# Layer-0 attention and feed-forward part joined in one block, normalisation per batch, and the opening of layer-1 attention reordered

## The chip, the core and the metric

One core of a Trainium2 chip runs the whole program. The metric is the device time of one execution in microseconds (us), the median of the runs shown. TensorE (PE in the rows) multiplies and transposes, VectorE (DVE) and ScalarE (ACT) do elementwise work, GpSimd (POOL) too, and SyncE (SP) issues the transfers from memory. Each has its own queue of instructions, worked through in order; semaphores tie the queues together.

## The reference

`x` is 8 batches of 128 tokens with 512 features. Four layers follow, each an attention part and a feed-forward part, each with a layer norm ahead of it and an addition behind:

```python
x = x + _L0_xattn_ref(_layernorm(x), ctx_4096, mask, position_bias, ...)   # 32 heads of 128
x = x + _L0_ffn_ref(_layernorm(x), W_org, lora_down, lora_up, lora_keys, Wq)
x = x + _L1_xattn_ref(_layernorm(x), ctx_4096, ctx_4096, Wq, Wk, Wv, Wo)   # 32 heads of 16, 8 for keys
x = x + _L1_ffn_ref(...)      # and two more layers
```

The feed-forward part of layer 0 projects the normalised x with `Wq`, takes the mean over the tokens of a batch, scores it against 8 keys, and uses the softmax of the scores as coefficients of 8 low-rank products (`lora_down`, `lora_up`), which are added to the dense product with `W_org`.

## The kernel before

Every operand of a large product is held as a high and a low part (`..._hi`, `..._lo`), and a product is three matmuls (`product`, lines 36 to 38). The high part is a rounding copy, mostly on ACT, the low part a subtraction on DVE or POOL.

`l0_attention` is one block with eight turns of four heads. In its last turn DVE also runs the last rounds of a ranking of the context (`rank_round`, `rank_end`) that only layer 2 needs. After the last turn PE makes the output product of the last two heads: `out_of_head(b, 0)` for six batches, then the last head's probabilities are transposed and weighed, then `out_of_head(b, 1)`. DVE adds each batch to x (line 879) and takes its statistics (`core.statistics`, line 87). All eight additions come behind the last ranking rounds in DVE's queue.

`l0_ffn` begins with the block of `norm_stage`: DVE aggregates the statistics of all eight batches (line 129), POOL raises the variances to the power -1/2 (line 153), DVE scales x into `xn` (line 134), PE transposes it (line 169), ACT and DVE write the high and low parts of `xt` (lines 182, 139). Meanwhile SP loads the first weights, ACT and POOL split them, and DVE makes the low part of the second half of `w_down` (line 927) at the end of its queue. A second block then makes the query (2 x 12 matmuls), the scores, eight low-rank products `low_rank(n)` of 12 matmuls and the output of 24 matmuls for each batch. A block begins on an engine when all engines have left the one before.

`l1_attention` is a third block. PE first projects keys and values from the context (`kt`, `vt`, 24 matmuls each), then transposes eight batches of `xn` (line 1184), then makes q (96 matmuls). DVE waits for ACT's high part of `kt`, subtracts (line 1344), and only then scales x into `xn` (line 1348). ACT splits `w_q` first, copies `kt`, `vt` and the eight `xt`, splits `w_o` (line 1297) and then copies q. POOL, after the power, splits `w_q` (line 1151), fills `v`, makes the four masked copies `kd` of the keys (line 1160) and splits `w_o`.

Of the kernel before, what the change touches and what calls it, by code (L numbers as in the profile page):

```python
# [12 lines left out]
P = 128  # L13
# [27 lines left out]
def as_f32(ap):  # L41
    return ap.bitcast(F32)


class Core:


    def __init__(self, nc, ctx):
# [24 lines left out]
        self.norms, self.split_norms, self.plain_norms = 0, 0, 0  # L73
# [34 lines left out]
def norm_stage(core, xn, xt, loads, act_first=None, pool_then=None, act_then=None, dve_then=None, banks=B,  # L108
# [3 lines left out]
    nc, n, n_split = core.nc, core.norms, core.split_norms  # L112
    core.norms += 1
    split = isinstance(xt, tuple)
# [4 lines left out]
    with nc.Block() as block:  # L119
# [6 lines left out]
        def _(dve):  # L126
# [5 lines left out]
            dve.wait_ge(core.rstd_done, n + 1)  # L132
# [18 lines left out]
        def _(pool):  # L151
            pool.wait_ge(core.var_done, n + 1)
# [42 lines left out]

L0_HEADS = 32
# [9 lines left out]
def l0_attention(core, dram):  # L206

    nc, x, bank = core.nc, core.x, core.bank
    with ExitStack() as ctx:
# [3 lines left out]

        qin = pair("qin", [P, DC, T])
# [3 lines left out]
        w_o = pair("w_o", [P, 2, D])  # L218
        raw_qk = [sb("raw_qk0", [P, 2, DC, P]), sb("raw_qk1", [P, 2, DC, P])]
        raw_v, raw_o = sb("raw_v", [P, DC, 2 * P]), sb("raw_o", [P, 2, D])  # L220
        q, k = sb("q", [P, T]), sb("k", [P, T])
        v_a = sb("v_a", [P, B, 2 * P])
        probs_t = sb("probs_t", [P, B, P])
        bias = sb("bias", [P, 2, P])
        comb = sb("comb", [P, B, P])
        neg = sb("neg", [P, B, P])
        top, row_sum, inv_sum = sb("top", [P, B]), sb("row_sum", [P, B]), sb("inv_sum", [P, B])
        idle = sb("idle", [P, 1])
        work, top8 = sb("work", [P, TPT, P]), sb("top8", [P, TPT, 8])
# [10 lines left out]
        probs = [sb("probs0", [P, B, P + 1]), sb("probs1", [P, B, P + 1])]  # L240

# [36 lines left out]
        OUT_LAST = ring_at(N - 1, "qk0")  # L278

# [10 lines left out]
        with nc.Block() as block:  # L290

            @block.sync
            def _(sp):
# [57 lines left out]
                turns(turn, sp)  # L351

            @block.gpsimd
            def _(pool):
# [53 lines left out]
                def turn(t, first, last):  # L408
# [13 lines left out]
                    if not last:  # L422
# [6 lines left out]
                turns(turn, pool)  # L429

            @block.tensor
            def _(pe):
# [149 lines left out]
                for b in range(B):  # L582
                    pe.wait_ge(h_drained, 2 * LAST + b // BH + 1)
                    if b >= 6:
                        pe.wait_ge(ring_drained, OUT_LAST + b - 5)
                        out_of_head(b, 0)
                    out_of_head(b, 1).then_inc(ring_full, 1)

            @block.scalar
            def _(act):  # L590
# [56 lines left out]
                def turn(t, first, last):  # L647
# [18 lines left out]
                    if last:  # L666
                        split_high(2 * t + 1, raw_o, w_o, o_loaded, o_hi, ring_at(t, "out_a") + 8)
# [9 lines left out]
                heads_high(LAST, 1)  # L677

            @block.vector
            def _(dve):  # L680
# [2046 lines left out]
```

## Time and profile before

| what | us |
| --- | --- |
| median of 3 runs | 1960.01 (1959.61 to 1960.69) |
| the profiled execution, its own time | 1959.41 |
| its span, first to last instruction | 1957.7 |
| PE busy | 1832.3 |
| DVE busy | 1379.4 |

The span is what the instructions of the core take; 1.7 us of the execution lie around it. In a timeline row the first number is the start in us from the span's start, the second what it or its group (x8) takes, and brackets name the idle time ahead of it and who ended it. The end of a matmul is modelled.

### The profile page before, as it was taken

What the parts mean: (1) busy time and instruction counts of PE and PEld (TensorE: products, weight loads), DVE (VectorE), ACT (ScalarE), POOL (GpSimd) and SP (SyncE); (2) the same over time, 40 slices, a digit from 0 to 9 for tenths busy, and PEclk for the clock granted to TensorE, in tenths of its full rate; (3) what the DMA queues carried; (4) which work ended last, traced back from release to release, by engine and by line L of the source; (5) the groups of instructions that cost most, each with busy time, mean ns of one, the idle gap of its engine ahead of it and who ended that gap; (6) DMA issues with size and microseconds to landing.
All of it is one profiled execution on the core that took longest, in us unless ns stands there. A gap on an engine that the chain in (4) does not pass through costs nothing. (4 is left out here: it accounts for less than half of the span.)

```text
span 1957.7 us, 28936 instructions
## 1 busy us (share of the span) xinstructions
PE 1832.3 (94%) x10418; PEld 1543.4 (79%) x10418; DVE 1379.4 (70%) x2796; ACT 611.0 (31%) x1712; POOL 604.2 (31%) x304
## 2 busy tenths in 40 slices
PE   7999999999999999996968979879889999999996
PEld 6888888888888888875855645666788888888885
DVE  5666666666666666676367855789788888888885
ACT  4321222221222212222025634531243333343330
POOL 6523333223333232303050005325334333243320
PEclk9999999999999999998989988989999999999998
DMA  4110111111111100102010003010101000010001
GB/s 166 59 37 20 43 50 47 50 47 50 47 50 47 42 28 26 50 14 81 0 43 1 1 11 97 22 39 22 44 22 44 33 32 32 32 43 32 32 12 55
DMA packets 29879, 78.43 MB, mean 40 GB/s; under 512 B 3857, under 2 KB 10705, under 8 KB 29425
## 3 DMA queue, kind: packets, MB, share of 16 engines
q1 hardware_dynamic: 29808, 77.50, 11.8%
q8 instruction: 44, 0.72, 0.2%
q14 instruction: 27, 0.21, 0.0%
HBM read 75.39 MB, written 2.10 MB: 40 GB/s over the span
## 5 line engine op out<-in xcount | busy, mean ns | idle before, releaser
L369 POOL TENSOR_TENSOR l0x_comb<-l0x_neg,l0x_bias 128x1024 f32<-128x1024 f32 x32 | 76.6, 2393 | 434.3 <-DVE l0x_probs L688 310.7
L609 ACT ACTIVATE l0x_probs_t<-bank 128x512 f32<-128x512 f32 x32 | 19.1, 597 | 546.2 <-PE bank L479 546.2
L2355 POOL TENSOR_TENSOR l3x_q<-l3x_q,l3x_cross 128x512 f32<-128x512 f32 x64 | 89.7, 1407 | 199.5 <-DVE l3x_q L1544 199.5
L38 PE MATMUL bank<-l0x_w_v_hi,ctx_lo 128*128 128x256 f32 x512 | 144.9, 283 | 0.0
L36 PE MATMUL bank<-l0x_w_v_hi,ctx_hi 128*128 128x256 f32 x512 | 144.9, 283 | 0.0
L37 PE MATMUL bank<-l0x_w_v_lo,ctx_hi 128*128 128x256 f32 x512 | 144.9, 283 | 0.0
L595 ACT ACTIVATE l0x_probs<-l0x_probs,l0x_top 128x129 f32<-128x129 f32 x256 | 99.4, 390 | 61.0 <-DVE l0x_top L692 61.0
L2486 ACT ACTIVATE l3x_probs<-l3x_probs,l3x_top 128x128 f32<-128x128 f32 x256 | 99.1, 389 | 37.4 <-DVE l3x_top L2555 37.3
L724 DVE TENSOR_TENSOR x<-x,bank 128x512 f32<-128x512 f32 x120 | 82.0, 683 | 38.7 <-PE bank L38 38.7
L361 POOL TENSOR_TENSOR l0x_w_qk_lo<-l0x_raw_qk,l0x_w_qk_hi 128x1024 fp32r<-128x1024 f32 x31 | 75.1, 2423 | 110.0 <-ACT l0x_w_qk_hi L602 110.0
L36 PE MATMUL bank<-l3x_qin_hi,l3x_w_q_hi 128*128 128x512 f32 x256 | 105.9, 414 | 3.1 <-PEq L119 3.1
L36 PE MATMUL bank<-ctx_hi,l0x_w_qk_hi 128*128 128x512 f32 x256 | 100.7, 393 | 8.1 <-DVE ctx_lo L799 8.1
L36 PE MATMUL bank<-l0x_qin_hi,l0x_w_qk_hi 128*128 128x512 f32 x256 | 105.3, 411 | 3.1 <-DVE l0x_qin_lo L823 1.6
L36 PE MATMUL bank<-l3x_w_o_hi,l3x_heads_hi 128*128 128x512 f32 x256 | 99.8, 390 | 1.5 <-issue 1.5
L38 PE MATMUL bank<-ctx_hi,l0x_w_qk_lo 128*128 128x512 f32 x256 | 100.6, 393 | 0.0
L37 PE MATMUL bank<-ctx_lo,l0x_w_qk_hi 128*128 128x512 f32 x256 | 100.6, 393 | 0.0
L37 PE MATMUL bank<-l3x_qin_lo,l3x_w_q_hi 128*128 128x512 f32 x256 | 100.5, 393 | 0.0
L38 PE MATMUL bank<-l0x_qin_hi,l0x_w_qk_lo 128*128 128x512 f32 x256 | 100.5, 393 | 0.0
L38 PE MATMUL bank<-l3x_qin_hi,l3x_w_q_lo 128*128 128x512 f32 x256 | 100.4, 392 | 0.0
L37 PE MATMUL bank<-l0x_qin_lo,l0x_w_qk_hi 128*128 128x512 f32 x256 | 100.2, 391 | 0.0
L37 PE MATMUL bank<-l3x_w_o_lo,l3x_heads_hi 128*128 128x512 f32 x256 | 99.6, 389 | 0.0
L38 PE MATMUL bank<-l3x_w_o_hi,l3x_heads_lo 128*128 128x512 f32 x256 | 99.6, 389 | 0.0
(464 smaller groups left out, 5250.3 us busy)
## 6 DMA issues: line engine op xcount, KB each, us to landing
l0x_raw_qk<-L_qk_dram SPq DMA_DIRECT2D x31, 512.0 KB, 4.3
l0x_raw_v<-L_v_dram SPq DMA_DIRECT2D x16, 512.0 KB, 5.5
l0x_raw_o<-L_o_dram SPq DMA_DIRECT2D x16, 512.0 KB, 5.4
l3x_raw<-L_q_dram SPq DMA_DIRECT2D x16, 512.0 KB, 3.5
l3x_raw<-L_o_dram SPq DMA_DIRECT2D x16, 512.0 KB, 3.5
kv_raw<-L_kv_dram SPq DMA_DIRECT2D x8, 512.0 KB, 3.5
l0x_ctx_raw<-ctx_t_dram SPq DMA_DIRECT2D x4, 512.0 KB, 5.8
x<-x_dram SPq DMA_DIRECT2D x8, 256.0 KB, 8.1
```

The source lines that it names most:

```text
L36: pe.matmul(out, lhs[0], rhs[0], start=start, stop=False)
L37: pe.matmul(out, lhs[0], rhs[1], start=False, stop=False)
L38: return pe.matmul(out, lhs[1], rhs[0], start=False, stop=stop)
L361: pool.tensor_tensor(f(w[1]), f(raw), as_f32(f(w[0])), ALU.subtract).then_inc(ready, 1)
L369: pool.tensor_tensor(comb[:, :, :], neg[:, :, :], bias[:, j:j + 1, :].to_broadcast([P, B, P]), ALU.add).then_inc(comb_ready, 1)
L595: act.activation(probs[j][:, b, :], probs[j][:, b, :], ACT.Exp, bias=top[:, b:b + 1], accum_out=row_sum[:, b:b + 1]).then_inc(exp_done, 1)
L609: act.activation(probs_t[:, 0:BH, :], bank[6][:, :].rearrange("p (b n) -> p b n", b=BH), ACT.Copy).then_inc(t_act, 1)
L724: dve.tensor_tensor(x[:, b, :], x[:, b, :], bank[b % 4][:, :], ALU.add).then_inc(ring_drained, 1)
L2355: pool.tensor_tensor(dst[:, part], dst[:, part], cross[n][:, :], ALU.add).then_inc(rotated, 1)
L2486: act.activation(probs[j % 2][:, b, :], probs[j % 2][:, b, :], ACT.Exp, bias=top[:, b:b + 1], accum_out=row_sum[:, b:b + 1]).then_inc(exp_ ...
```

## The change

The attention and the feed-forward part of layer 0 become one block, `l0_layer`. A helper `Handover` normalises x batch by batch: DVE takes the statistics and aggregates them behind each addition (`spread`), POOL does three small operations (`root`), ACT scales (`scale`), PE transposes (`turn`), ACT and DVE write the two parts (`high`, `low`). The order of these steps is written out on each engine. The first three weight pieces are loaded, and split by ACT and POOL, in the last attention turn; DVE splits none. The ranking rounds 3 to 6 and `rank_end` move from the last attention step to behind the additions of the feed-forward part (`rank_on`). PE's order at the start of that part becomes query half 0, low rank 0, query half 1, low rank 1. The banks of PSUM and the placing of tiles in SBUF change with it. In `l1_attention` DVE scales x before it subtracts `kt`; PE transposes four batches between `kt` and `vt`; ACT copies these ahead of `vt`, and splits `w_o` between the halves of q. Counters are renumbered.

```diff
+class Handover:
...
+    def spread(self, dve, b):
+        core = self.core
+        core.statistics(dve, b)
+        dve.wait_ge(core.stats_done, B * self.n + b + 1)
+        dve.bn_aggr(core.mv[:, b, :], core.stats[:, b, :]).then_inc(core.mv_done, 1)
+    def root(self, pool, b):
+        core = self.core
+        pool.wait_ge(core.mv_done, B * self.n + b + 1)
+        pool.tensor_scalar(core.var_eps[:, b:b + 1], core.mv[:, b, 1:2], EPS, None, ALU.add).then_inc(self.eps_done, 1)
+        pool.wait_ge(self.eps_done, b + 1)
+        pool.tensor_tensor(core.rstd[:, b:b + 1], core.var_eps[:, b:b + 1], core.neg_half[:, b:b + 1], ALU.pow
+                           ).then_inc(self.root_done, 1)
+        pool.wait_ge(self.root_done, b + 1)
+        pool.tensor_scalar(self.shift[:, b:b + 1], core.mv[:, b, 0:1], core.rstd[:, b:b + 1], -1.0, ALU.mult, ALU.mult
+                           ).then_inc(self.shift_done, 1)
+    def scale(self, act, b):
+        core = self.core
+        act.wait_ge(self.shift_done, b + 1)
+        if b >= self.ring:
+            act.wait_ge(core.xt_full, B * self.n + b - self.ring + 1)
+        act.activation(self.xn[:, b % self.ring, :], core.x[:, b, :], ACT.Identity, bias=self.shift[:, b:b + 1],
+                       scale=core.rstd[:, b:b + 1]).then_inc(core.xn_done, 1)
+    def turn(self, pe, b):
+        core = self.core
+        pe.wait_ge(core.xn_done, B * self.n + b + 1)
+        for c in range(DC):
+            mm = pe.transpose(self.bank_of(b)[:, c * P:(c + 1) * P], self.xn[:, b % self.ring, c * P:(c + 1) * P],
+                              core.ident[:, :])
+        mm.then_inc(core.xt_full, 1)
+    def high(self, act, b):
+        core = self.core
+        act.wait_ge(core.xt_full, B * self.n + b + 1)
+        act.activation(self.xt[0][:, :, b * P:(b + 1) * P], self.columns(b), ACT.Copy).then_inc(core.xt_hi, 1)
+    def low(self, dve, b):
+        core = self.core
+        dve.wait_ge(core.xt_hi, B * self.n_split + b + 1)
+        dve.tensor_tensor(self.xt[1][:, :, b * P:(b + 1) * P], self.columns(b),
+                          as_f32(self.xt[0][:, :, b * P:(b + 1) * P]), ALU.subtract).then_inc(core.xt_copied, 1)
...
+        self.norm = Handover(core, sem, xn, self.xt, lambda b: core.bank[(6, 7, 2, 3, 4, 5, 6, 7)[b]])
...
+    def low(self, pool, n):
+        pool.wait_ge(self.w_hi, n + 1)
+        pool.tensor_tensor(self.target(n, 1), self.raw_view(n), as_f32(self.target(n, 0)), ALU.subtract
+                           ).then_inc(self.core.l1_kv_split if n == 7 else self.by_pool, 1)
+    def sync(self, sp):
+        sp.dma_start(self.keys[:, :], self.dram["L0f_keys"]).then_inc(self.keys_loaded, 16)
+        for n in range(3, 8):
+            sp.wait_ge(self.by_pool, n - 2)
+            self.load(sp, n)
+    def gpsimd(self, pool):
+        for n in range(3, 8):
+            self.low(pool, n)
...
+        pe.wait_ge(self.by_pool, 1)
+        query_half(0)
+        pe.wait_ge(self.by_pool, 3)
+        pe.wait_ge(added, first_added + 6)
+        low_rank(0)
+        query_half(1)
+        pe.wait_ge(added, first_added + 7)
+        low_rank(1)
+        pe.wait_ge(self.keys_loaded, 16)
+        pe.wait_ge(self.query_done, 1)
...
+        for n in range(3, 8):
+            low_rank(n)
+        pe.wait_ge(self.by_pool, 7)
...
+            core.statistics(dve, b)
+            between(b)
...
+                sp.wait_ge(qk_ready[0], 2 * N - 1)
+                ffn.load(sp, 0)
+                sp.wait_ge(qk_ready[1], 2 * N)
+                ffn.load(sp, 1)
+                sp.wait_ge(v_ready, 2 * N)
+                ffn.load(sp, 2)
+                ffn.sync(sp)
...
+                    if last:
+                        for n in range(3):
+                            ffn.low(pool, n)
...
                 turns(turn, pool)
+                for b in range(B):
+                    ffn.norm.root(pool, b)
+                ffn.gpsimd(pool)
...
                 weigh_values(LAST, v_b, 1)
-                for b in range(B):
+                def last_out(b):
                     pe.wait_ge(h_drained, 2 * LAST + b // BH + 1)
                     if b >= 6:
-                        pe.wait_ge(ring_drained, OUT_LAST + b - 5)
+                        pe.wait_ge(ring_drained, ADDED + b - 6)
                         out_of_head(b, 0)
                     out_of_head(b, 1).then_inc(ring_full, 1)
+                def turn_x(b):
+                    if 2 <= b < 6:
+                        pe.wait_ge(ring_drained, ADDED + b)
+                    if b >= 6:
+                        pe.wait_ge(core.xt_copied, B + b - 5)
+                    ffn.norm.turn(pe, b)
+                for b in range(6):
+                    last_out(b)
+                turn_x(0)
+                turn_x(1)
+                last_out(6)
+                turn_x(2)
+                turn_x(3)
+                last_out(7)
+                for b in range(BH, B):
+                    turn_x(b)
+                ffn.tensor(pe, ring_drained, ADDED)
...
+                        act.wait_ge(ring_full, ring_at(t, "v_b") + 4)
+                        ffn.high(act, 0)
+                        act.wait_ge(ring_full, ring_at(t, "qk3") + 4)
+                        ffn.high(act, 1)
+                        ffn.high(act, 2)
...
+                norm.scale(act, 0)
+                norm.scale(act, 1)
+                norm.high(act, 0)
+                norm.scale(act, 2)
+                norm.high(act, 1)
+                norm.scale(act, 3)
+                norm.high(act, 2)
+                norm.high(act, 3)
+                norm.scale(act, 4)
+                norm.scale(act, 5)
+                norm.high(act, 4)
+                norm.scale(act, 6)
+                norm.high(act, 5)
+                norm.scale(act, 7)
+                norm.high(act, 6)
+                norm.high(act, 7)
+                ffn.scalar(act)
...
                 def last_step():
-                    i = 2 * N - 1
                     add_bias(LAST, 1)
                     copy_probs(LAST - 1)
-                    rank_round(i, 3)
...
                     heads_low(LAST - 1, 0)
                     normalise(LAST, 1)
-                    rank_round(i, 4)
                     copy_probs(LAST)
-                    rank_round(i, 5)
                     heads_low(LAST, 1)
-                    rank_round(i, 6)
-                    rank_end(i)
-                turns(turn, dve)
-                for b in range(B):
+                def add_last(b):
                     dve.wait_ge(ring_full, OUT_LAST + b + 1)
                     dve.tensor_tensor(x[:, b, :], x[:, b, :], bank[last_bank(b)][:, :], ALU.add).then_inc(ring_drained, 1)
...
+                    dve.wait_ge(ring_drained, ADDED + b)
+                    ffn.norm.spread(dve, b)
+                def rank_on(b):
+                    i = 2 * N - 1
+                    if 3 + b <= ROUNDS:
+                        rank_round(i, 3 + b)
+                    elif 3 + b == ROUNDS + 1:
+                        rank_end(i)
+                turns(turn, dve)
+                for b in range(BH):
+                    add_last(b)
+                norm = ffn.norm
+                norm.low(dve, 0)
+                norm.low(dve, 1)
+                add_last(4)
+                norm.low(dve, 2)
+                norm.low(dve, 3)
+                add_last(5)
+                add_last(6)
+                add_last(7)
+                for b in range(BH, B):
+                    norm.low(dve, b)
+                ffn.vector(dve, rank_on)
...
+                from_context(0, kt_full)
+                for b in range(BH):
+                    transpose_x(b)
+                from_context(1, vt_full)
+                pe.wait_ge(kt_done, 2)
+                transpose_x(BH)
+                transpose_x(BH + 1)
+                pe.wait_ge(vt_done, 2)
+                transpose_x(BH + 2)
+                transpose_x(BH + 3)
...
+                for b in range(BH):
+                    x_high(b)
...
+                for b in range(BH, B):
+                    x_high(b)
                 for half in range(2):
+                    if half == 1:
+                        act.wait_ge(raw_loaded, 32)
+                        act.activation(w_o[0][:, :, :], raw[:, :, :], ACT.Copy).then_inc(w_hi, 1)
...
+                dve.wait_ge(core.rstd_done, n_power + 1)
+                for b in range(B):
+                    dve.tensor_scalar(xn[:, b, :], core.x[:, b, :], core.mv[:, b, 0:1], core.rstd[:, b:b + 1],
+                                      ALU.subtract, ALU.mult).then_inc(core.xn_done, 1)
                 for half in range(2):
                     dve.wait_ge(kt_hi, half + 1)
                     dve.tensor_tensor(kt[1][:, half_of(half)], bank[half][:, :], as_f32(kt[0][:, half_of(half)]),
                                       ALU.subtract).then_inc(kt_done, 1)
...
-            l0_attention(core, dram)
             core.hold_kv(early)
-            l0_ffn(core, dram)
+            l0_layer(core, dram)
```

## Rows read from the trace of the kernel before

**Rows 1.** The page, busy time of TensorE: us, share of the span, instructions.

```profile
PE 1832.3 (94%) x10418; PEld 1543.4 (79%) x10418; DVE 1379.4 (70%) x2796; ACT 611.0 (31%) x1712; POOL 604.2 (31%) x304
```

**Rows 2.** Stretches: length, busy us of PE, PEld, DVE, ACT, POOL, granted clock, transfers.

```profile
884.10:893.20 9.10, 0.03 (x1) 0.03 (x1) 6.85 (x20) 0.51 (x1) 1.65 (x1) 0.67 0.25 67
...
904.60:936.40 31.80, 31.80 (x134) 25.31 (x135) 15.72 (x43) 5.64 (x8) 11.88 (x5) 0.95 0.24 83
936.40:979.90 43.50, 43.42 (x189) 35.07 (x187) 10.84 (x19) 0.00 (x0) 0.00 (x0) 1.00 0.00 0
...
992.80:1014.00 21.20, 7.57 (x32) 5.87 (x33) 21.20 (x13) 4.99 (x9) 17.01 (x6) 0.60 0.14 49
1014.00:1037.40 23.40, 23.40 (x104) 18.91 (x104) 7.27 (x12) 6.94 (x10) 4.62 (x1) 1.00 0.00 1
```

**Rows 3.** Waits of TensorE, 860 to 1060 us: total, times, longest.

```profile
PE bank L1184 <- DVE l1x_xn L1348: 13.4, 5, 3.1
PE bank L169 <- DVE l0f_xn L134: 9.2, 1, 9.2
PE bank L36 <- PEq L119: 5.6, 1, 5.6
```

**Rows 4.** Timeline of VectorE about the end of the attention.

```profile
875.98 0.69 DVE L719 TENSOR_TENSOR l0x_heads_lo<-bank,l0x_heads_hi 128x512 fp32r<-128x512 f32 x1 [0.29 <-ACT l0x_heads_hi L615]
...
879.03 0.68 DVE L879 TENSOR_TENSOR x<-x,bank 128x512 f32<-128x512 f32 x1
879.75 0.69 DVE L87 BATCH_NORM_STATS2 stats<-x 128x6 f32<-128x512 f32 x1
880.36 0.67 DVE L879 TENSOR_TENSOR x<-x,bank 128x512 f32<-128x512 f32 x1
...
901.98 2.28 DVE L927 TENSOR_TENSOR l0f_w_down_lo<-l0f_raw,l0f_w_down_hi 128x1024 fp32r<-128x1024 f32 x1
```

**Rows 5.** Timeline of TensorE, same stretch and after it.

```profile
876.73 0.50 PE L567 MATMUL bank<-l0x_w_o_hi,l0x_heads_hi 128*128 128x512 f32 x1 [0.52 <-DVE l0x_heads_lo L719]
...
904.58 0.76 PE L36 MATMUL bank<-l0f_xt_hi,l0f_w_q_hi 128*128 128x512 f32 x1 [5.56 <-PEq L119]
905.14 0.63 PE L37 MATMUL bank<-l0f_xt_lo,l0f_w_q_hi 128*128 128x512 f32 x1
...
907.69 0.39 PE L37 MATMUL bank<-l0f_xt_lo,l0f_w_q_hi 128*128 128x512 f32 x1
...
1006.41 1.12 PE L1184 MATMUL bank<-ident,l1x_xn 128*128 128x128 f32 x4 [2.62 <-DVE l1x_xn L1348]
```

**Rows 6.** POOL's small operations, all of the span: busy us, mean ns.

```profile
L153 POOL TENSOR_TENSOR rstd<-var_eps,neg_half 128x8 f32<-128x8 f32 x6 | 9.9, 1648 | 229.9 <-DVE var_eps L131 192.9 <-SPq L119 37.0
...
L1875 POOL TENSOR_TENSOR l2x_rs<-l2x_rs,neg_half 16x1 f32<-16x1 f32 x1 | 0.5, 542 | 9.0 <-DVE l2x_rs L2000 9.0
...
L1144 POOL TENSOR_TENSOR l1x_select<-l1x_same 128x4 f32<-128x4 f32 x1 | 0.2, 229 | 0.1
```

**Rows 7.** Timeline of ScalarE: a scaling and a high part.

```profile
26.55 0.81 ACT L619 ACTIVATE l0x_xr<-x,l0x_shift,l0x_r 128x512 f32<-128x512 f32 x1 [4.73 <-DVE l0x_shift L816]
...
1007.56 0.60 ACT L1294 ACTIVATE l1x_xt_hi<-bank 128x512 fp32r<-128x512 f32 x1 [3.14 <-PE bank L1184]
```

**Rows 8.** Timeline of TensorE, ScalarE, GpSimd and VectorE, opening of layer-1 attention.

```profile
981.60 0.47 PE L36 MATMUL bank<-ctx_hi,l_wkv_hi 128*128 128x512 f32 x1 [1.78 <-PEq L950]
...
986.53 1.92 ACT L1285 ACTIVATE l1x_w_q_hi<-l1x_raw 128x2048 fp32r<-128x2048 f32 x1 [67.63 <-DMA l1x_raw<-L1x_wq_dram]
...
982.52 1.64 POOL L1146 TENSOR_TENSOR rstd<-var_eps,neg_half 128x8 f32<-128x8 f32 x1
988.52 4.60 POOL L1151 TENSOR_TENSOR l1x_w_q_lo<-l1x_raw,l1x_w_q_hi 128x2048 fp32r<-128x2048 f32 x1 [4.36 <-ACT l1x_w_q_hi L1285]
...
990.17 21.30 DVE L1348 TENSOR_SCALAR l1x_xn<-x,mv,rstd 128x512 f32<-128x512 f32 x8
```

**Rows 9.** Timeline of VectorE in the next part: the same scaling with POOL idle.

```profile
1173.19 3.74 DVE L134 TENSOR_SCALAR l1f_xn<-x,mv,rstd 128x512 f32<-128x512 f32 x8 [1.76 <-POOL rstd L153]
```

More of the change, by code:

```diff
@@ L193, in _, with __init__, columns @@
                 act_then(act)
+class Handover:
+    def __init__(self, core, sem, xn, xt, bank_of):
+        self.core, self.xn, self.xt, self.bank_of = core, xn, xt, bank_of
+        self.ring = xn.shape[1]
+        self.n, self.n_split = core.norms, core.split_norms
+        core.norms += 1
+        core.split_norms += 1
+        self.shift = core.shift
+        self.eps_done, self.root_done, self.shift_done = sem("eps_done"), sem("root_done"), sem("shift_done")
+    def columns(self, b):
+        return self.bank_of(b)[:, :].rearrange("p (c t) -> p c t", c=DC)
+    def spread(self, dve, b):
[36 more added lines that the diff above has]
+                          as_f32(self.xt[0][:, :, b * P:(b + 1) * P]), ALU.subtract).then_inc(core.xt_copied, 1)
@@ L212, in l0_attention @@
         sem = lambda name: core.sem("l0x_" + name)
+        with ExitStack() as later:
+            ffn = L0Ffn(core, dram, later)
         qin = pair("qin", [P, DC, T])
@@ L240, in l0_attention @@
         probs = [sb("probs0", [P, B, P + 1]), sb("probs1", [P, B, P + 1])]
+        idle = sb("idle", [P, 1])
+        work, top8 = sb("work", [P, TPT, P]), sb("top8", [P, TPT, 8])
         x_loaded = [sem(f"x_loaded{b}") for b in range(B)]
@@ L278, in l0_attention @@
         OUT_LAST = ring_at(N - 1, "qk0")
+        ADDED = OUT_LAST + 1
         def last_bank(b):
@@ L426, in turn @@
                         split_qk(2 * t + 2, 1)
+                    if last:
+                        for n in range(3):
+                            ffn.low(pool, n)
                     split_low(2 * t + 1, raw_o, w_o, o_hi, o_ready)
                 turns(turn, pool)
+                for b in range(B):
+                    ffn.norm.root(pool, b)
+                ffn.gpsimd(pool)
             @block.tensor
@@ L1176, in _, with transpose_x @@
                         mm.then_inc(done, 1)
-                for b in range(B):
+                def transpose_x(b):
                     pe.wait_ge(core.xn_done, B * n_norm + b + 1)
-                    if b == BH:
-                        pe.wait_ge(kt_done, 2)
-                    if b == BH + 2:
-                        pe.wait_ge(vt_done, 2)
                     for c in range(DC):
@@ L1341, in _ @@
                 dve.tensor_scalar_add(core.var_eps[:, :], core.mv[:, :, 1], EPS).then_inc(core.var_done, 1)
+                dve.wait_ge(core.rstd_done, n_power + 1)
+                for b in range(B):
+                    dve.tensor_scalar(xn[:, b, :], core.x[:, b, :], core.mv[:, b, 0:1], core.rstd[:, b:b + 1],
+                                      ALU.subtract, ALU.mult).then_inc(core.xn_done, 1)
                 for half in range(2):
@@ L1345, in _ @@
                                       ALU.subtract).then_inc(kt_done, 1)
-                dve.wait_ge(core.rstd_done, n_norm + 1)
-                for b in range(B):
-                    dve.tensor_scalar(xn[:, b, :], core.x[:, b, :], core.mv[:, b, 0:1], core.rstd[:, b:b + 1],
-                                      ALU.subtract, ALU.mult).then_inc(core.xn_done, 1)
                 for b in range(B):
```

346 lines of the change are left out of this document (155 added, 191 removed).

## The prediction

> **What bounds the kernel now.** I read the page's busy times first: TensorE is busy for 94% of the span [rows 1], so only the stretches in which it isn't can give much. Then the stretches around the two joints that the change touches [rows 2]: from 884.1 to 893.2 us TensorE does nothing, and from 992.8 to 1014.0 it is busy 7.6 of 21.2 us, at a granted clock of 0.60. Then its waits [rows 3], which say whom it waits for: 9.2 us for the first normalised batch of the feed-forward part, 5.6 us at the border of the block behind `norm_stage`, and 13.4 us, in five pieces, for `l1x_xn`. Last the timelines of the engines that are late [rows 4 to 9].
>
> At the first joint everything is in series. The last output products could be added from 877.5 on, but VectorE is in the ranking rounds and adds the first batch at 879.03; an addition and its statistics take 1.33 us (879.03 to 880.36) [rows 4]; aggregation, power, scaling, transposes and splits of all batches follow, and at the end VectorE's share of `w_down`, 901.98 to 904.26, holds the block open. The query starts at 904.58 [rows 5].
>
> At the second joint the eight scalings take 21.30 us, from 990.17 to 1011.47 [rows 8]. The same eight take 3.74 us where POOL is idle [rows 9]. POOL is busy 17.0 of the 21.2 us of this stretch [rows 2], so most of the stall is VectorE and POOL together in SBUF, and the rest is that the scaling waits for `kt`, though x is ready long before.
>
> **The last attention turn.** Three loads (256, 512 and 512 KB) and three splits enter it. They wait in SP's queue behind the last load of the turn, on ACT in front of `w_o` and on POOL in front of `w_o`. TensorE is bound by its own products there, and `w_o` can't be split before the products that read its old value end anyway, so I cost them at nothing. If their cover fails, POOL's three splits (1.2 + 2.3 + 2.3 us by size from the 4.60 of `w_q` [rows 8]) could hold a VectorE operation with two SBUF inputs: VectorE's 2.28 us for 1024 columns of `w_down` beside a busy POOL [rows 4] are 1.1 over twice the 0.6 that 512 columns take elsewhere in those rows, so up to 1.1 us for each of two such operations. SP then waits for POOL before each further load; nothing of the attention is queued behind it.
>
> The ranking rounds leave the last step. They delayed the low part of the heads a little; I take 0.3 us (0 to 1): TensorE's `out_of_head(0, 1)` starts at 876.4 instead of 876.73 [rows 5].
>
> **The handover, step by step.** Six last products of 3 matmuls take 0.7 us each, so batch 0 is complete at 877.3. VectorE ends the second low part of the heads at the same time: two of 0.69 us from 875.98 on [rows 4], 0.2 between them, 0.3 earlier.
>
> - VectorE per batch: addition to statistics 0.72 us, statistics to aggregation 0.72 (the wait for its own result, of the same form), aggregation 0.1, which no row shows alone: 1.53. Additions 0 to 3 end, aggregated, at 883.5; low parts 0 and 1 to 885.1; addition 4 to 886.7; low 2 and 3 to 887.9; additions 5, 6, 7 to 892.5.
> - POOL's `root`: the power takes 1.65 us for 8 columns and 0.54 for one [rows 6]; two more small operations at 0.23 [rows 6] and three hops of 0.05 (876.67 to 876.73 from VectorE to TensorE [rows 4, 5]) make 1.15. It isn't shown for 128x1 with a column of scalars: 0.8 if each is a hop and 0.1, 2.1 if the power costs its 1.65 whatever its width. I take 1.15, since the one-column row is nearest. Below the 1.53 of VectorE it is latency only.
> - ACT's `scale`: 0.81 us [rows 7]. TensorE's `turn`: 1.12 at the low clock [rows 5]. `high`: 0.60 [rows 7].
>
> The last batch goes 892.5 + 1.15 + 0.85 + 1.15 = 895.7, and then the query starts, for the first half's low parts are there since 888. Batches 0 to 3 and `last_out(6)`, `last_out(7)` fill TensorE between 881 and 887.6; nobody waits for the last two longer than VectorE takes to come to them. `w_down` is split since 855. **Gain: 904.6 - 895.7 = 8.9 us**, 6 to 11 by the bounds: 1 for POOL, 1.5 for the hops, and 2 the other way if the statistics' wait is shorter.
>
> **The rest of the feed-forward part.** The products are the same 24 + 96 matmuls, so 904.6 to 936.4 becomes 895.7 to 927.5 [rows 2]. The order query 0, low rank 0, query 1, low rank 1 puts one more product (2.8 us) behind the scores; nothing waits longer. Later pieces: `w_org` is split on ACT at 896.3 to 898.2 and POOL until 902, `w_up` and `w_kv` behind the exponential, on POOL until some 918; TensorE asks for them at 927. The ranking rounds, 1.05 us each behind four additions, lie where VectorE is busy 10.8 of 43.5 us [rows 2]: nothing.
>
> **The opening of layer-1 attention**, on the old clock (subtract 8.9). The power ends at 984.16, the scaling starts at once and takes 3.74 us: 987.9. POOL takes up `w_q` at 988.52, because ACT waits for the transfer until 986.53 [rows 8]. So the scaling is over 0.6 us before POOL starts, and `kt`'s subtraction starts when it did. TensorE: at 104 instructions in 23.4 us [rows 2] `kt` lasts from 981.6 to 987.2, four transposes of batches at full clock (half of 1.12) 989.2, `vt` 994.7, four more 996.7, and q, for which `w_q` is split at 993.1. Before, q started at 1014.0. **Gain: 17.3 us.** The keys' masked copies on POOL start as before and are through before 1014, for the row from 1014.0 on has just one POOL instruction, `w_o` [rows 2]; the scores need them 23.4 us after the start of q, at 1020. `w_o` on ACT (1.9 us) sits between two copies of q 2.8 us apart.
>
> Here a rule says why. The Trainium skill, SBUF — State Buffer, Who interferes with whom: VectorE in a two-port mode, which `tensor_scalar` can enter, and GpSimd take the same pair of ports by turns, each for a whole instruction, and whoever issues first gets it. By that rule one scaling passes per POOL instruction, and the trace agrees: 21.3 us for eight. It also says what a small shift would do, which is a rival below.
>
> **Sum:** the profiled execution's span 1957.7 - 8.9 - 17.3 = 1931.5; with the 1.7 around it 1933.2. The median of the runs lies 0.6 above the profiled execution: **1934 us**.
>
> **Rivals.**
>
> 1. *Scaling and POOL still collide (0.09).* The margin is 0.6 us. If the scaling starts late, or `w_q` arrives early, the last scalings wait for POOL. One caught: it ends at 993.1, `kt` is subtracted by 994.5, and nothing is lost. Two caught: the second ends behind the filling of `v`, at 995.4, `kt` at 996.8, 2 us lost. All eight caught would give back up to 15. For it: 0.6 us is little. Against: both starts hang on the same block border. Time 1936 to 1948.
> 2. *The handover doesn't run ahead (0.07).* If each hop between engines costs 1 us more than here, four hops and three stages waiting in written-out order eat most of 8.9. Time about 1942. Against: a hop in the rows took 0.06 us [rows 4, 5].
> 3. *The clock stays low (0.04).* TensorE is less busy between 881 and 895.7. At the low clock a matmul of 512 columns follows the last in 0.43 us, at the high in 0.23 [rows 5]. Before, seven were slow, then it was granted fully; I count the same seven. If all of query 0 and two low ranks were slow: 36 x 0.2 = 7 us: 1941.
> 4. *Slower than before (0.02).* The same mechanism on the other side: to lose 26.2 us takes 131 slow matmuls, that is the query, all low ranks and more. The decision is whether the clock comes back within 131 matmuls; in the row it came after seven.
> 5. *Nothing gained (0.02):* what was saved waits later, for instance at the masked keys of the second joint and at `w_up` at the first.
>
> **Numbers.** The forecast has 0.76, its own range 1929 to 1938. 1929 to 1942 takes in the milder half of rivals 1 to 3 and leaves about 0.15 out. A difference of 0.2%, 4 us, is about what a measurement of this kernel can tell from no change. Faster 0.96, within 0.02, slower 0.02.
>
> **What the profile after would show.** The addition of batch 0 at about 877.3 and a distance of 1.5 us between additions; `root`'s power at 0.5 to 0.6 us; the first query matmul at 895 to 897, with some slow ones behind it; `l1x_xn` x8 in 3.7 us, ended before POOL's `w_q`; no wait for `l1x_xn` on TensorE over 0.5 us; q 15.1 us behind the first `kt` matmul instead of 32.4. The prediction is wrong if the scalings stretch again, if TensorE waits for `xn` in every turn, or if an engine that I cost at nothing, ACT in its written-out order above all, becomes the last one.

## The result and the profile after

The changed kernel takes 1925.48 us (median of 4 runs, 1923.58 to 1926.27), the kernel before, run beside it, 1959.81 (4 runs): a ratio of 0.9823, 95% interval 0.9806 to 0.984. The profiled execution has 1925.09 us and a span of 1923.4. So the change is faster by 34.3 us, the sign is as forecast, and the time lies 8.5 us below the forecast and 3.5 below the lower end of its range. Two runs of the kernel before that stood beside the experiments p1 to p4 took 2656 and 4689 us; every median here leaves such slow runs out.

Where it came from, by landmarks on TensorE in the two profiled executions. A turn is here the work on two heads, which ends in 48 output products; there are 16 of them, and the sixteenth is cut in two, `out_of_head(b, 0)` and `out_of_head(b, 1)`. Each row of the table runs from the landmark of the row above it to its own.

| stretch | before | after | gain | forecast |
|---|---|---|---|---|
| first output product of attention turn 1 to that of turn 15 | 750.15 | 744.41 | 5.74 | 0 |
| from there to `out_of_head(0, 0)` | 19.33 | 18.65 | 0.68 | 0 |
| to `out_of_head(0, 1)`, start of the last products | 8.14 | 9.67 | -1.53 | 0.3 |
| to the query's first product | 27.85 | 19.41 | 8.44 | 8.6 |
| to the first `w_org` product | 30.92 | 30.01 | 0.91 | 0 |
| to layer 1's first `kt` product | 46.10 | 45.46 | 0.64 | 0 |
| to the first q product | 32.40 | 14.46 | 17.94 | 17.3 |
| to the scores | 23.96 | 23.96 | 0 | 0 |
| to the end of the span | 919.7 | 918.2 | 1.5 | 0 |

The page of after, busy time of TensorE (us, share of the span, instructions): as many instructions as in [rows 1], 10.2 us less busy.

```profile
PE 1822.1 (95%) x10418; PEld 1541.8 (80%) x10418; DVE 1357.4 (71%) x2786; ACT 616.3 (32%) x1720; POOL 613.0 (32%) x328
```

Waits of TensorE in after, 855 to 1030 us (total, times, longest). The waits of [rows 3] for `l1x_xn` and behind `norm_stage` are gone; of the 9.2 us for the first normalised batch 6.3 are left, in seven pieces. The last row is the border of the block ahead of layer 1.

```profile
PE bank L242 <- ACT l0f_xn L235: 6.3, 7, 2.1
...
PE bank L36 <- PEq L537: 1.8, 1, 1.8
```

The joint in after, timeline of VectorE, POOL, ScalarE and TensorE.

```profile
872.87 0.69 DVE L1174 TENSOR_TENSOR x<-x,bank 128x512 f32<-128x512 f32 x1 [0.17 <-PE bank L827]
873.60 0.70 DVE L88 BATCH_NORM_STATS2 stats<-x 128x6 f32<-128x512 f32 x1
874.33 0.18 DVE L217 BATCH_NORM_AGGREGATE mv<-stats 128x2 f32<-128x6 f32 x1
874.42 0.66 DVE L1174 TENSOR_TENSOR x<-x,bank 128x512 f32<-128x512 f32 x1
...
875.94 0.66 DVE L1174 TENSOR_TENSOR x<-x,bank 128x512 f32<-128x512 f32 x1
...
874.60 0.24 POOL L222 TENSOR_SCALAR var_eps<-mv 128x1 f32<-128x1 f32 x1 [16.43 <-DVE mv L217]
874.93 0.58 POOL L224 TENSOR_TENSOR rstd<-var_eps,neg_half 128x1 f32<-128x1 f32 x1
875.61 0.26 POOL L227 TENSOR_SCALAR shift<-mv,rstd 128x1 f32<-128x1 f32 x1
...
875.91 0.81 ACT L235 ACTIVATE l0f_xn<-x,shift,rstd 128x512 f32<-128x512 f32 x1 [3.93 <-POOL shift L227]
...
886.54 0.81 ACT L235 ACTIVATE l0f_xn<-x,shift,rstd 128x512 f32<-128x512 f32 x1 [1.90 <-POOL shift L227]
...
887.50 1.09 PE L242 MATMUL bank<-ident,l0f_xn 128*128 128x128 f32 x4 [2.08 <-ACT l0f_xn L235]
...
890.53 1.09 PE L242 MATMUL bank<-ident,l0f_xn 128*128 128x128 f32 x4 [0.43 <-ACT l0f_xn L235]
891.27 0.78 PE L36 MATMUL bank<-l0f_xt_hi,l0f_w_q_hi 128*128 128x512 f32 x1
...
893.86 0.40 PE L36 MATMUL bank<-l0f_xt_hi,l0f_w_q_hi 128*128 128x512 f32 x1
```

The reader sees the chain that was forecast: VectorE takes up the first addition after waiting 0.17 us for its product, the next additions follow 1.55 and 1.52 us behind, POOL's three operations take 1.27 us, and the query starts at 891.27, 0.74 us behind the start of the last transposes (890.53). Behind the first batch the largest wait of ScalarE is the 1.90 us at batch 5, and TensorE waits 2.08 us for what it scales there (887.50): VectorE makes two low parts between the additions of batches 4 and 5.

The opening in after, timeline of VectorE and POOL: eight scalings in 3.75 us, which end 0.30 us before POOL takes up `w_q`.

```profile
969.37 3.75 DVE L1492 TENSOR_SCALAR l1x_xn<-x,mv,rstd 128x512 f32<-128x512 f32 x8 [1.78 <-POOL rstd L1280]
973.86 1.29 DVE L1496 TENSOR_TENSOR l1x_kt_lo<-bank,l1x_kt_hi 128x512 fp32r<-128x512 f32 x2 [0.75 <-ACT l1x_kt_hi L1430]
...
973.42 4.63 POOL L1285 TENSOR_TENSOR l1x_w_q_lo<-l1x_raw,l1x_w_q_hi 128x2048 fp32r<-128x2048 f32 x1 [4.09 <-ACT l1x_w_q_hi L1427]
```

What the forecast doesn't have is the first line of the table. In every attention turn the 48 output products `bank<-l0x_w_o,l0x_heads` are 0.36 us shorter. Summed by kind of product over the fourteen turns of that line, they take 152.35 us instead of 157.38, and that is 5.0 of the 5.7; the products of `l0x_qin` with `l0x_w_qk` take 158.18 instead of 158.93, and all others are the same within 0.1. In the kernel before, the first and the last of a turn's 48 (timeline of TensorE, turn 15) start 11.01 us apart:

```profile
849.26 0.39 PE L36 MATMUL bank<-l0x_w_o_hi,l0x_heads_hi 128*128 128x512 f32 x1
...
860.27 0.40 PE L38 MATMUL bank<-l0x_w_o_hi,l0x_heads_lo 128*128 128x512 f32 x1
```

In after, the same two, 10.65 us apart:

```profile
843.54 0.39 PE L36 MATMUL bank<-l0x_w_o_hi,l0x_heads_hi 128*128 128x512 f32 x1
...
854.19 0.39 PE L38 MATMUL bank<-l0x_w_o_hi,l0x_heads_lo 128*128 128x512 f32 x1
```

No line of the loop around them changed. What changed is where the tiles lie: one tile of 32 bytes a partition (`core.shift`) was added in front of nearly all others, and the tiles of the attention stand in another order.

### The profile page after: what moved, and what is told of

The parts are those of the page before. It is cut to its first block and busy times, and to the rows that moved or that the text cites. A ratio compares the mean times of both kernels' runs of the same rounds, so it can differ in the third digit from the quotient of the medians.

```text
span 1923.4 us, 28949 instructions
## 1 busy us (share of the span) xinstructions
PE 1822.1 (95%) x10418; PEld 1541.8 (80%) x10418; DVE 1357.4 (71%) x2786; ACT 616.3 (32%) x1720; POOL 613.0 (32%) x328
```

## The experiments

In the code cuts the word in brackets says which kernel an experiment starts from, and the rest is what it changes. "Turns 1 to 15" is the first landmark stretch of the table (750.15 before, 744.41 after). It depends on no scatter of the start or the end. Addresses are bytes within a partition, worked out from the order and sizes of the tiles. Medians of different experiments come from different sessions, in which the kernel before took 1958.15 to 1960.05 us, so a difference of 1 or 2 us between two of them is read from a stretch and not from the times.

### Four shifts by 32 bytes

```
p1  (before)   + self.sb(ctx, "pad_core", [P, B])       all tiles by 32
p2  (before)   + sb("pad_a", [P, B])  heads  + sb("pad_b", [P, B])
p3  (before)   both
p4  (after)    as p2
```

> The kernel before, with one unused tile of 32 bytes a partition ahead of nearly all others: everything behind it moves up by 32 bytes, w_o from 32 to 0 and the heads from 0 to 32 (remainder of the address by 64 bytes). The 48 output products of two heads took 11.01 us before and 10.65 after the change. Theory P, that the two operands of a matmul have to lie at the same remainder: they still differ, 11.0 us, 1960 in all. Rival M, that the moving operand (w_o) has to lie at a multiple of 64: 10.65 us and 1954. Rival N, that placement plays no part: 11.0 us, 1960, here and in the next two.

> The kernel before, with 32 unused bytes ahead of the two heads tiles and 32 behind: the heads alone change their remainder, from 0 to 32, where w_o lies already. Theory P (same remainder): 10.65 us for 48 products, so 16 x 0.36 = 5.7 us less, 1954. Rival M (moving operand at a multiple of 64): w_o is still at 32, so 11.0 us and 1960. Rival N: 1960.

> The kernel before with both paddings: w_o at 0 and the heads at 0 (32 + 32), as in the changed kernel. Theory P and rival M: 10.65 us for 48 products, 1954. Rival N: 1960. In the feed-forward part of layer 0 the pairs change sides too: xt from 32 to 0, w_down from 0 to 32, so P expects nothing gained there.

> The changed kernel with 32 unused bytes ahead of and behind the heads tiles: w_o at 0, heads at 32. Theory P: 11.0 us for 48 products and 5 to 6 us more than the changed kernel's 1925.5, 1931. Rival M: w_o stays at 0, 10.65 us and 1925.5. Rival N: 1925.5.

The difference is that of the addresses of `w_o` and `heads` modulo 256, taken the shorter way round (160 counts as 96).

| kernel | difference, bytes | first to last of 48 products, us | turns 1 to 15, us | median, us |
|---|---|---|---|---|
| before | 96 | 11.01 | 750.15 | 1959.62 |
| p1 | 96 | 11.01 | 749.90 | 1957.84 |
| p2 | 128 | 10.92 | 749.10 | 1958.37 |
| p3 | 128 | 10.92 | 748.72 | 1957.92 |
| p4 | 32 | 10.96 | 749.33 | 1929.33 |
| after | 0 | 10.65 | 744.41 | 1925.48 |

p4 shows that placement is the cause: 32 bytes under one tile pair of the changed kernel give back 4.9 of the 5.7 us. p2 and p3 missed what was expected of them, 10.65 us, and p3 overthrows a rule modulo 64, for there both tiles have the remainder 0, as in after, and little is gained. What is left to test is the difference of the two operands modulo 256. (In time p1 to p3 are within 0.13% of the kernel before, ratios 0.9991, 0.9995 and 0.9987: the stretch shows what the median can't.)

### The rule modulo 256, in both kernels

```
q1  (before)   + sb("pad_a", [P, 40])  heads  + sb("pad_b", [P, 24])    difference 0
q2  (after)    + sb("pad_a", [P, 32])  heads  + sb("pad_b", [P, 32])    difference 128
```

> The kernel before with 160 unused bytes ahead of the heads tiles and 96 behind, so that the heads have the remainder 224 by 256 bytes, as w_o has. Theory Q: the 48 output products are the faster the nearer the two operands lie in their remainders by 256: difference 96 gave 11.01 us, 32 gave 10.96, 128 gave 10.93, 0 (changed kernel) 10.65. It expects 10.65 us here and 16 x 0.36 = 5.7 us less, 1954. Rival P' (only the remainder by 64 counts, the rest is the new order of the tiles): 10.93 us, as where the heads moved by 32.

> The changed kernel with the heads tile 128 bytes further on, so that it and w_o lie 128 apart modulo 256 instead of 0; everything behind it stays where it was. If the equal remainder modulo 256 is what made the output products short, 48 of them take 10.92 to 10.96 us again instead of 10.65 (as in the kernel before and in all runs with a difference of 32, 96 or 128), sixteen times over, and the time is 4 to 5 us above the changed kernel's, 1929.5 to 1930.5. If what mattered was where heads lies by itself (its remainder modulo 128 is unchanged here), or w_o by itself, they stay at 10.65 and the time stays at 1925.5.

q1: 10.66 us, turns 1 to 15 in 744.67, time 1953.91 (1959.5 beside it; ratio 0.9971, interval 0.9952 to 0.9991). q2: 10.93 us, 748.57, time 1930.97. Moved alone in the kernel before, the tile brings 5.5 of the 5.7 us. The output products give 5.0 of these, as in after. The rest, 0.4 in q1 and 0.75 in after, lies in the products of `l0x_qin` with `l0x_w_qk`, whose operands lie 0 apart in every one of these kernels; p1, in which all tiles move together, has 0.3 there too. What shortens those is open. (q2: the median was expected at 1929.5 to 1930.5 and came at 1930.97.) The two products of q1 (timeline of TensorE), 10.66 us apart:

```profile
843.96 0.39 PE L36 MATMUL bank<-l0x_w_o_hi,l0x_heads_hi 128*128 128x512 f32 x1
...
854.62 0.39 PE L38 MATMUL bank<-l0x_w_o_hi,l0x_heads_lo 128*128 128x512 f32 x1
```

### The same rule in the feed-forward part and in layer 1

In the kernel before `w_down` and `w_org` lie 32 from `xt`, in after 0. `w_q` of the feed-forward part lies 0 from it in both; r1 moves it along. In both `w_q` of layer 1 lies 128 from its `xt`.

```
r1  (after)       xt  + sb("pad_x", [P, 8])  w_down w_q ...  gap 424 -> 416
r2  (after)       xn  + sb("pad_o", [P, 8])  w_org w_up h
s1  (h2, below)   layer 1: + sb("pad_x", [P, 32])  xt kt vt ...  + sb("pad_i", [P, 32])  a at
```

> The changed kernel with the feed-forward part's w_down and w_q 32 bytes further on (the gap behind them 32 bytes shorter), so that they lie 32 from xt modulo 256, as w_down does in the kernel before, where it is 0 in the changed one. If the rule of equal remainders holds in this part too, 96 low-rank products and 24 query products go from about 0.226 us back to 0.234, 0.8 to 1.2 us in all, the stretch from the query's first product to the first kt product of the next layer goes from 75.5 back to 76.3 to 77.0, and that accounts for most of the 1.5 us by which it shrank; time 1926.3 to 1926.7. If the rule is only of the attention's tiles, spacing and stretch stay, and the 1.5 us come from elsewhere (the order of query and transposes, other adds).

> The changed kernel with w_org, w_up and h of the feed-forward part 32 bytes further on: w_org then lies 32 from xt modulo 256, as in the kernel before, instead of 0; w_up and h keep their difference of 0. If the placement shortened the w_org products as it did the low-rank ones, the stretch from the first w_org product to the next layer's first kt product goes from 45.46 back to 46.0 to 46.2 (46.10 in the kernel before), and the w_up products in it stay the same; time 0.6 us above the changed kernel's. If those 0.64 us came from VectorE's additions or from waits instead, the stretch stays at 45.4 to 45.5.

> The version with all last adds first, and in the second layer's attention xt moved by 128 bytes, so that it and w_q lie 0 apart modulo 256 instead of 128. If the rule holds where it was not looked for, the 96 products of q follow each other in 0.227 us instead of 0.230 to 0.232 and q to scores is 23.4 to 23.7 us instead of 23.96; time 0.3 to 0.5 us below that version's, 1921.3. If 128 apart is harmless for these, 23.96 stays.

| | difference, after or h2 -> this kernel | start to start of two products, mean, ns | stretch, us |
|---|---|---|---|
| r1, low rank | 0 -> 32 | 227 -> 233 | query to `w_org` 30.01 -> 30.60 |
| r2, `w_org` | 0 -> 32 | 227 -> 233 | `w_org` to `kt` 45.46 -> 46.14 |
| s1, q of layer 1 | 128 -> 0 | 232 -> 227 | q to scores 23.96 -> 23.47 |

All three went the way that the rule says. r2 and s1 came inside their ranges; r1 gave back 0.6 us from the query to `kt` (76.09 instead of 75.48) where 0.8 to 1.5 were expected. The times can't show 0.6 us: r2 took 1925.03, and r1 1923.83, 2.5 below what was expected of it. s1 takes 1919.77 (1919.5 to 1921.14), ratio to the kernel before 0.9803, interval 0.9786 to 0.9819: the fastest of all.

### The opening of layer 1 alone

```
o1 (before)  the whole new l1_attention, counters as in before
o2 (before)  DVE: scale x8, then kt_lo      (only this)
o3 (before)  POOL: + pool.wait_ge(core.xn_done, B * (n_norm + 1))  ahead of split_low(0, w_q)
j1 (after)   the whole old l1_attention
```

> The kernel before with the new layer-1 attention alone. If the two halves of the change add up, q starts 14.5 us behind the first kt matmul instead of 32.4 and the whole is 17.9 us faster, 1942. If the opening lives on the joint ahead of it, less.

> The kernel before with one thing of the new opening: VectorE scales x before it subtracts kt. PE and ACT keep their old order. Theory: the collision with POOL was the whole stall, so the scaling takes 3.7 us instead of 21.3; TensorE transposes all eight batches behind vt and q starts 16 to 17 us earlier (15.5 to 16 us behind the first kt matmul), 1943. Rival: the interleaved transposes and ACT's order carry half of it, so q starts only 9 us earlier, 1951.

> The kernel before, old order everywhere, but POOL waits for the eight scalings before it splits w_q. Theory, that VectorE's tensor_scalar and POOL shut each other out: the scaling starts at 990.2 as before and takes 3.7 us, POOL's split ends at 998.5, and q starts then, 17 us behind the first kt matmul: 15.4 us less, 1944. Rival, that it is the place in VectorE's queue alone: the scaling still takes 21 us, POOL starts later and the time goes up by 10 to 20 us.

> The changed kernel with the second layer's attention opening of the kernel before (VectorE's and GpSimd's old order); handover and placement stay. If the opening is independent of the rest, its whole 17.3 to 17.9 us come back: 1942.8 to 1943.4, and kt to q is 32.4 us again. If handover and opening share a wait, less comes back.

| | `kt` to q | time |
|---|---|---|
| before | 32.40 | 1959.5 to 1960 |
| o1 | 14.44 | 1942.58 |
| o2 | 14.94 | 1945.3 (1 run) |
| o3 | 16.85 | 1945.93 (1 run) |
| j1 | 32.25 | 1942.50 |
| after | 14.46 | 1925.48 |

The parts add up: o1 is 16.9 us faster than the kernel before beside it, j1 17.0 slower than after. o2 and o3 were expected at 1943 and 1944 and took 2 us more; in both profiled executions TensorE has a stretch of low clock far ahead of the opening, told of below, that costs 2.8 and 1.5 us. o3 leaves the old order, in which the scaling comes behind `kt`, and only keeps POOL out. Timeline of VectorE and POOL in o3:

```profile
991.93 1.29 DVE L1345 TENSOR_TENSOR l1x_kt_lo<-bank,l1x_kt_hi 128x512 fp32r<-128x512 f32 x2 [6.36 <-ACT l1x_kt_hi L1289]
993.14 3.74 DVE L1349 TENSOR_SCALAR l1x_xn<-x,mv,rstd 128x512 f32<-128x512 f32 x8
...
996.96 4.56 POOL L1151 TENSOR_TENSOR l1x_w_q_lo<-l1x_raw,l1x_w_q_hi 128x2048 fp32r<-128x2048 f32 x1 [9.66 <-DVE l1x_xn L1349]
```

The 21.30 us of [rows 8] become 3.74. So 15.5 of the 17.9 us are the two engines getting out of each other's way. Of what is left most is the price of this cure: q starts at 1001.6, with the end of POOL's delayed split (996.96 + 4.56). VectorE's order alone (o2), two groups of lines exchanged, does the same without delaying `w_q` and brings 1.9 us more, and the new orders of TensorE and ScalarE the last 0.5.

### The handover, one piece at a time

```
h1 (after)  PE: ffn.query_half(pe, 0) ahead of turn_x(4..7)
h2 (after)  PE: last_out(0..7), then turn_x(0..7);  DVE: add_last(0..7), then low(0..7)
h3 (after)  rank_round 3 to 6 and rank_end back in the last attention step
h4 (after)  POOL and ACT: pieces 0 to 2 split behind root / behind the norm, not in the last turn
k1 (after)  h1 and h2 together
```

> The changed kernel, with the first half of the query (12 matmuls, which need the first four batches only) between the output product of batch 7 and the transposes of batch 4. Theory, that TensorE only waits for VectorE's and ACT's chain from 883.4 to 891.3 us: the 12 matmuls lie in that wait, the last transpose stays where it was, and the low-rank products start 2.8 to 4 us earlier: 1922. Rival, that the chain itself is delayed by the transposes of batch 4 coming later: nothing gained, 1925.

> The changed kernel, with VectorE making all eight additions first and the eight low parts behind them, and TensorE all eight output products first. Theory, that the last batch's chain (addition, root, scale, transposes) sets the start of the query and that the four low parts inside VectorE's chain delay it: the last aggregation comes at 885.0 instead of 888.1, the query starts at 888.2 instead of 891.3, 3.1 us less, 1922.4. Rival, that ACT's order of scalings and high parts is the bound: the query starts within 1 us of 891.3.

> The changed kernel with the ranking rounds back in the last attention step, none in the feed-forward part. Theory: the first addition waits for a round and the end of the ranking, 1.5 us, and the heads for 0.3: 1.8 us more, 1927.3. Rival, that the rounds lie in waits there as well: 1925.5.

> The changed kernel with the first three weight pieces loaded early but split late: on ACT behind the last high part of x, on POOL behind the last root. Theory: the query waits for POOL's first piece until 894.2, the low-rank products for the third until 899 instead of starting at 895.2: 3.7 us more, 1929.2. Rival, that the splits would have been hidden anyway: 1925.5.

> Both handover edits together: the last adds and all eight last output groups first, then the transposes, and the query's first half ahead of the last four transposes. If each fills a different wait, the gains add (3.4 and 3.7 us below the changed kernel): 1918.3. If they fill the same wait of TensorE, which first waits for the scaled batches and then for ScalarE's copies, the pair is worth no more than the better one: 1921 to 1922. My expectation is between, 1919 to 1921: the low-rank products begin 17 to 19 us after the last output products begin, instead of 23.4 (changed kernel), 20.2 (adds first) and 19.1 (query between).

Measured from the start of `out_of_head(0, 1)`:

| | to the query | to the first low-rank product | time |
|---|---|---|---|
| before | 27.85 | 34.86 | 1959.81 |
| after | 19.41 | 23.37 | 1925.48 |
| h1 | 11.93 | 19.06 | 1922.06 |
| h2 | 16.80 | 20.20 | 1921.72 |
| h3 | 21.16 | 25.51 | 1926.75 (2 runs) |
| h4 | 22.31 | 27.60 | 1928.91 (2 runs) |
| k1 | 15.76 | 25.01 | 1926.90 |

The ranking rounds ahead of the additions cost 1.75 us on this path, the late weights 2.9 up to the query and 4.2 up to the low rank. In h4 (timeline of ScalarE, POOL and TensorE) the query waits for POOL's low part of `w_q`. POOL itself waited 3.31 us for ScalarE's high part, which now stands behind the last high part of x. The query then comes in at the low clock, and its twelve products start 0.43 us or more apart throughout:

```profile
890.47 0.62 ACT L322 ACTIVATE l0f_w_q_hi<-l0f_raw 128x512 fp32r<-128x512 f32 x1
...
891.17 1.27 POOL L326 TENSOR_TENSOR l0f_w_q_lo<-l0f_raw,l0f_w_q_hi 128x512 fp32r<-128x512 f32 x1 [3.31 <-ACT l0f_w_q_hi L322]
...
892.49 0.80 PE L36 MATMUL bank<-l0f_xt_hi,l0f_w_q_hi 128*128 128x512 f32 x1 [2.56 <-POOL l0f_w_q_lo L326]
893.09 0.63 PE L37 MATMUL bank<-l0f_xt_lo,l0f_w_q_hi 128*128 128x512 f32 x1
```

h1 and h2 are 3.4 and 3.8 us below after in time, and k1 is 1.4 above it, where I had expected some 5 gained. The times alone don't carry this: as ratios to the kernel before beside them they are 0.9817, 0.9812 and 0.9826, each with an interval of some 0.0017 to both sides that holds the 0.9823 of after. The traces do: from `out_of_head(0, 1)` to the first `w_org` product it is 49.4 us in after, 45.2 in h1, 46.2 in h2 and 51.2 in k1. Timeline of TensorE and ScalarE in k1:

```profile
888.03 0.77 PE L36 MATMUL bank<-l0f_xt_hi,l0f_w_q_hi 128*128 128x512 f32 x1 [4.93 <-DVE l0f_xt_lo L254]
888.59 0.63 PE L37 MATMUL bank<-l0f_xt_lo,l0f_w_q_hi 128*128 128x512 f32 x1
...
893.29 1.38 PE L242 MATMUL bank<-ident,l0f_xn 128*128 128x128 f32 x8
...
897.28 0.48 PE L36 MATMUL bank<-l0f_xt_hi,l0f_w_down_hi 128*128 128x512 f32 x1
...
894.27 0.60 ACT L249 ACTIVATE l0f_xt_hi<-bank 128x512 fp32r<-128x512 f32 x1 [9.14 <-PE bank L242]
894.77 0.80 ACT L235 ACTIVATE l0f_xn<-x,shift,rstd 128x512 f32<-128x512 f32 x1
```

With the additions first, the low parts of batches 0 to 3 come only at 885.4 to 887.9, and the query's first half, now ahead of the last transposes in PE's queue, waits 4.93 us for them. The transposes of batches 4 and 5, whose inputs are ready, stand behind it. ScalarE waits 9.14 us for the first of them and only then scales batch 6 (894.77). And after the idle time the twelve query products follow each other in 0.43 us instead of 0.23. The query ahead of the transposes pays only while VectorE makes the first low parts early, and with all additions first it makes them late.

## Why the prediction was right in sign and 8 us too high

**The step that failed** is the sum 1957.7 - 8.9 - 17.3, which has no term for the products themselves. The prediction kept their length ("TensorE is bound by its own products there" in the attention, "The products are the same 24 + 96 matmuls" in the feed-forward part) and so put the placing of the tiles, which the change names, at nothing, without a reason and without a bound. The products became shorter. Turns 1 to 15 gained 5.7 us, 5.0 of them in the output products (q1 has 5.5 by one tile's place alone; p4 and q2 take 4.9 and 4.2 back), the low-rank products some 0.6 (r1) and `w_org` 0.7 (r2).

**What else lies between.** Of the 0.68 us behind turn 15, 0.36 are its own 48 output products. The span came 8.1 us below its forecast: 6.4 up to `out_of_head(0, 0)`, 1.55 in the rest of the feed-forward part, 0.6 in the opening and 1.5 behind the scores, less 1.8 in `out_of_head(b, 0)` and 0.2 in the handover.

**What ran against it.** 1.53 us were lost again in `out_of_head(b, 0)`. TensorE was granted half its clock there, the 1.2 GHz level, in the profiled execution of after (windows: length, busy us of PE, PEld, DVE, ACT, POOL, granted clock, transfers):

```profile
862.00:864.00 2.00, 1.81 (x6) 1.51 (x7) 1.43 (x3) 0.00 (x0) 0.00 (x0) 0.75 0.00 0
864.00:866.00 2.00, 2.00 (x6) 1.52 (x6) 0.00 (x0) 0.00 (x0) 0.00 (x0) 0.50 0.00 0
866.00:868.00 2.00, 2.00 (x9) 1.55 (x8) 0.00 (x0) 0.00 (x0) 0.00 (x0) 0.90 0.00 0
```

Of the 20 profiled executions 9 have this dip (9.4 to 10.9 us instead of 8.0 to 8.2), of kernels with and without the change, so I don't put it down to the change. What decides it is open: TensorE did the same ahead of it with the dip and without. The window ahead of the stretch, first in after, then in h4, which has no dip:

```profile
860.00:862.19 2.19, 0.17 (x2) 0.03 (x1) 1.99 (x4) 1.59 (x9) 0.00 (x0) 1.00 0.00 0
...
860.00:862.12 2.12, 0.10 (x1) 0.03 (x1) 1.99 (x4) 1.51 (x8) 0.00 (x0) 1.00 0.00 0
```

In both TensorE is all but idle for 2 us, and busy 16.39 of the 17.00 us before that.

**The handover** was right: 8.44 for 8.6. Its terms held: the addition of batch 0 started 1.01 us behind the first last product (0.9 forecast), additions 1.52 to 1.55 apart (1.53), POOL's column 1.27 (1.15, inside 0.8 to 2.1). The splits of weights in the last turn were rightly costed at nothing, and h4 shows what they cost when they come late. I counted seven slow query products; five started 0.43 us or more ahead of the next, and one 0.31. Two side readings of mine were off and entered no sum: [rows 4] has 0.67 to 0.69 us for 512 columns and not 0.6, so `w_down` is 0.9 us over twice that and not 1.1; and the upper bound of POOL's column is 2.26 by its own terms, not 2.1.

**The rest of the feed-forward part** was to give nothing and gave 1.55: 0.6 and 0.7 by placement. The rest, 0.3, fits two slow products fewer (2 x 0.2), which no run takes apart.

**The opening** was right: 17.94 for 17.3. o3 confirms the reason by itself. With POOL kept out, the same eight scalings in the same place take 3.74 us instead of 21.30. By the rule cited in the prediction (the Trainium skill, SBUF — State Buffer, Who interferes with whom) a VectorE instruction in a two-port mode and a GpSimd instruction shut each other out for the whole of the one that was issued first. The trace agrees in the main, though no row shows which mode the scalings were in, and the prediction read it too simply ("one scaling passes per POOL instruction ... 21.3 us for eight"). Taken one by one in the trace of before, only five of the eight scalings were held up: the first took 4.97 us and ended at 995.14, behind both POOL's split of `w_q` and its filling of `v`; the next four took 3.81 to 3.82, each ending 0.3 us behind one of POOL's four copies of the keys; the last three, with POOL idle, took 0.53 to 0.54. So rival 1's price for one caught scaling, an end at 993.1 and nothing lost, was too low.

**Rivals.** Rival 1 didn't happen, but its margin was 0.30 us and not 0.6. Rival 2 didn't: the hops were as short as taken. Rival 3 didn't at the query, with five slow products; the clock was low in another place, above. Rivals 4 and 5 didn't. All five asked what could be given back; none asked what else the change could bring, and so the range had 8 us above the forecast and 5 below.

**Behind the scores** 1.5 us were gained that belong to nothing: over all 20 profiled executions this stretch takes 916.1 to 919.8 us, and before and after lie within that, at 919.7 and 918.2.

## What to carry to other kernels

When a change adds, drops or reorders tiles, write down for each heavy product the addresses of its two operands modulo 256, before and after, and give a difference a price; here it was 6 to 7 ns for each product of 512 columns. A kernel whose TensorE is busy 94% of the time is not out of reach: 5 us lay in its operands' placement, for two pads. When two engines hold each other up in SBUF, let the short instructions finish before the long one is issued, and look at the margin that is left. An order written out by hand on one engine is tied to the order on the others: two reorderings that gain alone can lose together.

## What the runs showed of the hardware

In a long row of 128x512 fp32r matmuls at the full clock, one follows the other in 0.227 us where the stationary and the moving operand lie at equal addresses modulo 256; with a difference of 32, 96 or 128 it takes 0.232 to 0.234. Seen for four pairs (`w_o` with `heads`, `w_down` and `w_org` with `xt`, `w_q` with layer 1's `xt`), switched on or off by pads alone in five kernels (p4, q1, q2, r1, r2) and forecast in a sixth (s1). A difference of 0 is not enough in a short row: behind matmuls of another kind the first two to nine distances are 0.224 to 0.236 us there too, and the very first 0.31 or more. In after the products of `l0x_qin` with `l0x_w_qk` from 63.97 us on take 0.315, then 0.231, 0.231, 0.236, 0.228, 0.233, 0.231 and then 0.227, and layer 1's output products `bank<-l1x_w_o,l1x_at`, six in a row and 0 apart, have a median of 0.233. What in the chip does this no run shows. Differences other than 0, 32, 96 and 128, other widths and other types weren't tried.
